# The additions that GpSimd makes between indirect transfers, taken out of the first retention phase

## The reference, cut to what matters

```python
h = _L0_tok_ref(x, L0_tok_conv_w)      # out[b,t,:] = sum over k of conv_w[:, token[b, t+k-1], k]
h = h + _L0_attn_ref(_layernorm(h, axis=-1), ...)   # xpos, 8 heads, scores * decay, relu
# first half of h = h + _L0_ffn_ref(_layernorm(h, axis=-1), ...):
gate_probs = jax.nn.softmax(x @ gate_w + gate_b, axis=-1)
top_v, top_i = jax.lax.top_k(gate_probs, K)          # K = 2 of 8 experts for each token
```

## Time and profile before

| | before |
|---|---|
| median of 3 runs | 2166.8 us |
| the profiled execution, its own time | 2167.65 us |
| its span in the profile | 2165.9 us |
| POOL busy | 1242.7 us |
| additions L353 | 384, 184.1 us |
| scatters L345 | 256, 264.2 us |
| gathers L333 | 128, 127.3 us |
| mean granted clock of TensorE | 0.964 of full speed |

### The profile page before, as it was taken

One profiled execution on the slowest core, in us unless ns is written; L12 is line 12 of the kernel. 1 busy time (PEld: TensorE's weight loads), 2 busy tenths in 40 slices (PEclk: granted clock), 3 DMA queues, 4 the chain that ended last, 5 costly groups with the idle time before them and its releaser, 6 DMA issues. The chain is left out here.

```text
span 2165.9 us, 58044 instructions
## 1 busy us (share of the span) xinstructions
PE 1961.8 (91%) x19420; PEld 1463.7 (68%) x19420; DVE 1521.3 (70%) x4436; ACT 1339.7 (62%) x2844; POOL 1242.7 (57%) x1563
## 2 busy tenths in 40 slices
PE   5888888888888599999999959999999699999997
PEld 2555555555555377777777736777777599999997
DVE  4978888888887333333333359999998688888877
ACT  3756566665655222222222249999899598998885
POOL 5488888888876788878887821112112033333334
PEclk9999999999998699999999969999999899999999
DMA  3112122121210365555555523111110011111111
GB/s 100 40 58 69 60 65 64 60 66 57 67 55 30 113 169 160 164 162 163 164 163 161 149 78 133 40 39 39 39 45 14 15 36 40 41 41 41 41 41 35
DMA packets 113820, 168.89 MB, mean 78 GB/s; under 512 B 19234, under 2 KB 66747, under 8 KB 113572
## 3 DMA queue, kind: packets, MB, share of 16 engines
q1 hardware_dynamic: 87940, 105.22, 17.5%
q0 software_dynamic: 25760, 62.09, 9.1%
HBM read 121.92 MB, written 45.32 MB: 77 GB/s over the span
## 5 line engine op out<-in xcount | busy, mean ns | idle before, releaser
L1259 ACT ACTIVATE b_hT<-b_hbank,b_w 128x512 f32<-128x512 f32 (+1 forms) x156 | 98.2, 630 | 320.0 <-PE b_hbank L1229 256.3
L1203 POOL DMA_INDIRECT done<-b_y,b_row x270 | 263.6, 976 | 48.5 <-issue 44.0
L345 POOL DMA_INDIRECT sent<-a_xn_mid,a_pos_cur x256 | 264.2, 1032 | 42.3 <-issue 41.3
L1285 DVE TENSOR_SCALAR b_hT<-b_hbank,b_w 128x512 f32<-128x512 f32 (+1 forms) x156 | 105.7, 677 | 228.5 <-PE b_hbank L1229 203.4
L1239 PE MATMUL b_bank<-b_w,b_hT 128*128 128x128 f32 x2160 | 254.2, 275 | 1.0 <-DVE b_hT L1285 1.0
L1239 PEld LDWEIGHTS b_bank<-b_w,b_hT 128*128 128x128 f32 x2160 | 247.5, 192 | 1.2 <-DVE b_hT L1285 1.2
L1229 PE MATMUL b_hbank<-b_xT,b_w 128*128 128x512 f32 (+1 forms) x624 | 247.1, 539 | 0.8 <-ACT b_xT L1266 0.8
L1492 POOL TENSOR_TENSOR c_k_early<-c_xn,c_k_decay 64x512 f32<-64x512 f32 x32 | 40.7, 1273 | 340.3 <-ACT c_xn L1699 340.3
L353 POOL TENSOR_TENSOR tv<-tv 128x128 f32<-128x128 f32 x384 | 184.1, 479 | 61.8 <-DVE a_pos_cur L894 50.3
L1229 PEld LDWEIGHTS b_hbank<-b_xT,b_w 128*128 128x128 f32 x624 | 113.4, 192 | 87.5 <-issue 83.1
L1202 POOL TENSOR_TENSOR b_spacer<-b_fill 128x192 f32<-128x192 f32 x270 | 139.9, 518 | 47.9 <-DVE b_y L1293 40.0
(11 more groups left out here) (247 smaller groups left out, 4575.7 us busy)
## 6 DMA issues: line engine op xcount, KB each, us to landing
b_w<-pack_dram SPq DMA_DIRECT2D x78, 258.0 KB
b_w<-pack_dram SPq DMA_DIRECT2D x78, 256.0 KB
c_rows<-done SPq DMA_DIRECT2D x32, 512.0 KB, 3.8
b_x<-sent SPq DMA_DIRECT2D x57, 260.0 KB
d_b_all<-b_rows SPq DMA_DIRECT2D x32, 256.0 KB, 3.4
out_dram<-h_all SPq DMA_DIRECT2D x32, 256.0 KB, 2.3
b_b<-pack_dram SPq DMA_DIRECT2D x78, 64.5 KB
tv<-tv_dram SPq DMA_DIRECT2D x1, 4736.0 KB, 16.2
```

Source lines behind the costliest of these rows:

```text
L345: pool.indirect_dma_start(out=sent_d, out_offset=bass.IndirectOffsetOnAxis(ap=pos_cur[:, g.par, b, k:k + 1], axis=0), in_=xn_mid[:, g.par, ...
L1203: pool.indirect_dma_start(out=done_d, out_offset=bass.IndirectOffsetOnAxis(ap=row[:, s.k, j:j + 1], axis=0), in_=y[:, s.par, j, :], in_off ...
```

## The change

The function `space_out` and its calls go, and the tile `spare` with its memset. The semaphore `ids_step`, which counted the copy and four additions of each step, becomes `ids_ready`, which counts the copies alone; `pool_step` counts one increment for each group. Waits for data and the order of gathers and scatters stay.

```diff
@@ take_ids, gather
-                                 ids[:, bass.ds(g.n * GB, GB)]).then_inc(ids_step, 1)
+                                 ids[:, bass.ds(g.n * GB, GB)]).then_inc(ids_ready, 1)
-                pool.wait_ge(ids_step, g.n * (GB + 1) + 1)
+                pool.wait_ge(ids_ready, g.n + 1)
                 if g.is_past(2):
                     pool.wait_ge(h_ready, g.n - 1)
                 take_ids(g.after())
                 for b in range(GB):
-                    space_out(spare[:, 1, :], ids_step, g.n * (GB + 1) + (b + 2))
                     pool.indirect_dma_start(
@@ scatter
                     if i == 0:
                         pool.wait_ge(placed, g.n + 1)
-                    space_out(spare[:, 0, :], pool_step, g.n * (2 * GB) + (i + 2))
+                        pool.sem_inc(pool_step)
                     pool.indirect_dma_start(
@@
-            def space_out(x, step, n):
-                pool.wait_ge(step, n)
-                pool.tensor_tensor(x, x, x, ALU.add).then_inc(step, 1)
-            pool.memset(spare, 0.0).then_inc(pool_step, 1)
             pool.wait_ge(ids_loaded, 16)
-            pool.wait_ge(pool_step, 2)
+            pool.wait_ge(pool_step, 1)
```

More of the change, by code:

```diff
@@ L122, in retention_phase @@
 def retention_phase(nc, h_all, w_all, routing, sent_d, ids_d, table_d, wq_d, wqs_d, wkkv_d,
-                    gn_w_d, gn_b_d, tabs_d, tabs_c_d, gate_w_d, gate_c_d, slot_c_d, tags_d, spare):
+                    gn_w_d, gn_b_d, tabs_d, tabs_c_d, gate_w_d, gate_c_d, slot_c_d, tags_d):
     with ExitStack() as ctx:
@@ L235, in retention_phase @@
         consts = sem("consts")
-        ids_step = sem("ids_step")
+        ids_ready = sem("ids_ready")
         tok_made = sem("tok_made")
@@ L368, in _ @@
                 pool.wait_ge(scattered[i], (NG // 2) * (2 * GB) * 16)
-            pool.wait_ge(pool_step, NG * (2 * GB) + 2)
-            pool.wait_ge(ids_step, NG * (GB + 1) + 1)
+            pool.wait_ge(ids_ready, NG + 1)
         @block.tensor
@@ L2961, in build @@
                        routed.enter_context(nc.sbuf_tensor("ident_b", [P, P], F32)))
-            spare = tv[:, 0:2, :]
             retention_phase(nc, h_all, w_all, routing, sent, a["ids"].bitcast(U32), a["table"], a["wq"],
                             a["wqs"], a["wkkv"], a["gn_w"], a["gn_b"], a["tabs"], a["tabs_c"], a["gate_w"],
-                            a["gate_c"], a["slot_c"], a["tags"], spare)
+                            a["gate_c"], a["slot_c"], a["tags"])
             experts_phase(nc, routing, sent, done, a["pack"], a["fill_tags"])
```

## The result

| | before | changed | ratio |
|---|---|---|---|
| median of 4 runs | 2166.53 us | 2360.49 us | 1.0889, interval 1.0866 to 1.0912 |
| profiled execution | 2167.65 us | 2357.86 us | |
| its span | 2165.9 us | 2355.9 us | |
| granted clock, mean | 0.964 | 0.918 | |

The changed kernel is slower by 8.9%, outside the range of the prediction (2100 to 2300). The page of the changed kernel: busy time by engine, then the 40 slices of DVE and POOL.

A forecast was written before the change was run, and what follows sets the result against it. POOL was taken as the bound of the first retention: -7.8 + 9.8 = +2.0 us a group, +52 over 26 steps, tail +4.5, start +0.4, together +57 on 2167.65: 2225 us. The 8-in-10 range was 2100 to 2300.

The forecast's parts named there:

- POOL is full before: First retention, 100 to 640 us: POOL accounts for 516 of 540 us, so its twelve transfers set a group's time.
- What goes, 7.8 us a group: On POOL, twelve additions at 0.487 us and twelve gaps at 0.163 us leave each group.
- The price of a transfer behind another, 1.91 us: Eleven of twelve transfers on POOL rise from 1.02 to 1.91 us, +9.8 us a group.
- the two ends: Bounds for a following transfer's price on POOL: 0.99 us, nothing extra, to 3.1 us, waiting until the one before landed.
- the 1.73 at which I had put the turn: Transfer price in us on POOL under which removing the additions pays.
- the tail: Last 16 scatters of the phase: -9.3 us for additions and gaps, +13.8 for dearer transfers, together +4.5 us.
- At the start: First four gathers, awaited by TensorE until 12.15 us: four additions less, three dearer transfers, together +0.4 us.
- Rival 1: Back-to-back transfers cost nothing extra, VectorE bounds the first retention at 19.0 us a step: 2103 us, up to 2116; chance 0.35.
- Rival 3: POOL's transfers go one at a time until landed, 3.1 us each: near 2580 us; 0.07 together with prices over 2.3.
- The time of the other engines, put at nothing: DVE, ACT, PE and SP keep their instructions; no cost was entered for them.
- The direction, slower: Whole kernel: chance 0.57 of slower, against 0.35 faster and 0.08 the same.
- The rule weighed: GpSimd SBUF reads and two-input DVE instructions exclude each other; blocks falling on transfers instead: 1.0 us per group at most.

The follow-up runs named there:

- memset_only: The changed kernel plus one 128x1536 fill of the scratch tile at the phase's start: 2097.4 us, 0.9673 of the kernel before.
- run_of_eight: The kernel before with two additions a group, 672 columns each, ahead of the eight scatters and the four gathers: 2124.5 us, 0.9791.

## Why the prediction was wrong

**POOL is full before: right.** Twelve times 64 columns more cost 31 us, and on chip 2 each cut of POOL's time gained until a step was near 19 us. (Two of the digits that the prediction took as 8 at the edges of slices 2 to 11 are 7; nothing hangs on it.)

**What goes, 7.8 us a group: right in the sum, if the gaps are booked elsewhere.** The twelve additions went, 5.8 us: POOL's busy time in a step falls to 12.4 us (memset_only 12.3), where 15.7 and 19.3 stand in the earlier trace rows. The gaps ahead of the transfers, 2.0 us, stayed, and behind another transfer they grew from 0.16 to 0.30; they are in the price that follows.

**The price of a transfer behind another, 1.91 us: the first step that failed.** It is 1.27 us from start to start, 0.97 plus a gap of 0.30, in the changed kernel and in all others alike; with the disturbed ones the mean is (239.2 + 100.8 + 61.9 + 28.0) / 336 = 1.28 us in memset_only. I had taken it from the longest rows, the first of them beside a VectorE instruction, and one transfer doesn't hold up the next in that way; of the two ends the price lay near the low one. With the measured price the sum of a group is -7.8 + 11 x (1.28 - 1.02) = -4.9 us, and the sign turns: the price is under the 1.73 at which I had put the turn. In the tail of the changed kernel, the last sixteen scatters took 20.6 us (899.55 to 920.18) instead of 26.3, -5.7 for my +4.5. At the start, TensorE began at 10.98 us instead of 12.15, -1.2 for my +0.4.

**Rival 1, nothing extra and VectorE the bound, 2103 us: right for POOL, and the step right in memset_only,** at 0.35. Its point was a price up to 1.48. In memset_only the steps run from 91.27 to 578.97 us:

```profile
91.27 0.68 DVE L735 TENSOR_TENSOR h_all<-a_bank,a_rows 128x512 f32<-128x512 f32 x1
...
578.97 0.68 DVE L735 TENSOR_TENSOR h_all<-a_bank,a_rows 128x512 f32 x1
```

That is 487.7 / 26 = 18.76 us for the 19.0 forecast, and 2097.4 us for 2103. The waits for gathered rows are gone, as it said. That it is VectorE that sets this step isn't shown: it is busy for 17.26 of 18.84 us, TensorE for 17.73, and no run took work from VectorE while POOL had room. Had the changed kernel's results come in time, the answer to the change would, by memset_only, have been faster by 3%.

**Rival 3, one at a time until landed: refuted.** POOL doesn't wait for the landing, 3.1 us in the earlier trace rows: in a run of eight, transfers start 1.27 us apart in run_of_eight, memset_only and the changed kernel, but where one takes 1.4 us or more. The estimate from the Trainium skill's page, DMA: Bandwidth & Descriptors, 2.15 us for each scatter in a row, isn't what POOL pays.

**The time of the other engines, put at nothing: the second step that failed, and the one that made the 2360.** "DVE, ACT, PE and SP keep their instructions" stood there without a price. They kept them, but TensorE's results reached ScalarE and VectorE up to 6.7 and 11.2 us late, 364 us of idle time by the rows that end in "remote", and a step took 27.9 us where I had 23, and where memset_only, with the same transfers and nothing late, takes 18.8. I had asked what the change does to POOL and its transfers, and not whether the transfers could touch the link between two other engines. No row of before could have shown it. Why the results are late stays open.

**The direction, slower, was luck.** Of the +190 us none is POOL's: POOL lost 184 us of work, and waited for the others. By my own sum with the measured price the kernel would have been faster. I had also written that the start-to-start time of the scatters "decides everything". It doesn't: it is 1.27 us in the changed kernel and in memset_only, 263 us apart.

**The rule weighed** (Trainium skill, SBUF — State Buffer, who interferes with whom): I gave 1.0 us a group for blocks that might fall on transfers instead of additions. The mean of a transfer is 1.012 us in memset_only ((239.2 + 100.8) / 336) against 1.02 before, so nothing was passed on. VectorE has 17.26 us of work in a step instead of 17.48 to 17.88, as the rule has it when fewer instructions of POOL read SBUF.

## What to carry to other kernels

Spacers between indirect transfers are worth their time only where something else needs them: here two additions of one column, or none, save 3% against twelve of 128 on the chips where they were tried, while on another chip every thinning of the twelve cost time. When two engines that the edit didn't touch begin to wait for each other, look in the waits for a releaser that the profile can't name, and compare the end of the work awaited with the start of the waiting one. And run the kernel under study itself in every batch, on each chip, before reading a series of variants as a series.

## What the runs showed of the hardware

- An indirect transfer right behind another starts 1.27 us after it, 0.97 of work and a gap of 0.30; behind an addition the gap is 0.16. Its place in the row makes no difference, up to eight scatters.
- TensorE's results can reach ScalarE and VectorE 1 to 7 us late (11.2 at most) in a phase in which POOL issues indirect transfers, where 0.03 to 0.15 us is the rule; the result of VectorE looked at in the same time (345.82) came after 0.10. The profile mostly calls the releaser "remote". It was seen on one chip of three in the experiments, and in the changed kernel.
- An addition of one column on POOL takes 0.19 us, one of 128 columns 0.41 undisturbed, one of 288 0.66.
- While the engines waited for late results, TensorE's granted clock was 0.81 and 0.87 in a step, between the two levels of 1.2 and 2.4 GHz, and the sixteen matmuls of L490 took 3.62 us (351.46); in the step of memset_only the clock was 1.00, and they took 2.05 (318.74).
